# Layer 3's rank products in four partition groups side by side, with two sets of four PSUM banks

## The reference

```python
def _L3_ffn_ref(x, W, b, A, Bmat, LiMEs):     # RANK = 32, 8 experts
    scaling = ALPHA / RANK                    # 0.5
    H = jnp.einsum('btd,od->bto', x, W) + b
    z = jnp.einsum('btd,dr->btr', x, A)
    ...
    weights_full = jnp.repeat(weights, N_GRAM, axis=1)
    p_mix = jnp.einsum('bte,er->btr', weights_full, LiMEs)
    delta = jnp.einsum('btr,ro->bto', z * p_mix, Bmat) * scaling
    return H + delta
x = x + _L3_ffn_ref(_L3_cond_ref(x, itok_B_9_3973, L3_cond_conv_w), L3_ffn_W, L3_ffn_b, L3_ffn_A, L3_ffn_Bmat, L3_ffn_LiMEs)
```

## Time and profile before

| | us |
|---|---|
| median of 3 runs | 1017.63 |
| lowest and highest of them | 1017.13, 1018.17 |
| the profiled execution, device time | 1017.95 |
| its span in the trace | 1016.2 |
| TensorE busy in the span | 931.9 (92%) |
| VectorE busy | 573.8 (56%) |
| layer 3's stretch from the last rank product of the softmax on | 953.4 to 1016.2 |

### The profile page before, as it was taken

One profiled execution on the slowest core, in us unless ns is written; L12 is line 12 of the kernel. 1 busy time (PEld: TensorE's weight loads), 2 busy tenths in 40 slices (PEclk: granted clock), 3 DMA queues, 4 the chain that ended last, 5 costly groups with the idle time before them and its releaser, 6 DMA issues.

```text
span 1016.2 us, 9968 instructions
## 1 busy us (share of the span) xinstructions
PE 931.9 (92%) x3113; PEld 483.7 (48%) x3114; DVE 573.8 (56%) x883; ACT 389.2 (38%) x444; POOL 87.8 (9%) x125
## 2 busy tenths in 40 slices
PE   0499968999899999999999999999899999898998
PEld 0495428997344444444444444444244344443332
DVE  7889968887999999888840000000214224255352
ACT  2025627878777776666631010000012222241100
POOL 4100007600000000000000000022010100100000
PEclk9999998999999999999999999998899999999899
DMA  6863234560000000000010010140100000000021
GB/s 224 291 219 104 104 131 161 210 219 28 21 21 17 28 29 2 28 28 1 0 40 0 1 54 1 41 154 0 42 0 1 0 1 1 0 1 1 22 83 62
DMA packets 32591, 60.12 MB, mean 59 GB/s; under 512 B 5730, under 2 KB 7986, under 8 KB 31458
## 3 DMA queue, kind: packets, MB, share of 16 engines
q1 hardware_dynamic: 31842, 59.45, 17.3%
q0 software_dynamic: 704, 0.10, 0.1%
HBM read 51.07 MB, written 8.47 MB: 59 GB/s over the span
## 4 chain that ended last, share of the span: by engine, by line
PE 75%; DVE 17%; issue 3%; ACT 3%; ACTq 1%; DMA 1%; DVEq 1%; SPq 0%
PE ps L781 73%; DVE acc L1305 4%; DVE T L1305 3%; ACT above L632 2%; DVE W2T L1305 1%; PE ps L821 1%; ACTq L651 1%; DVE raw L1283 1%; DVE amax L1276 1%; DVE W2T L1147 1%; PE ps L1011 1%; DVE X L1372 1%; DVE W2T L1153 1%; DVE W2T L1150 0%; DVEq L1368 0%
## 5 line engine op out<-in xcount | busy, mean ns | idle before, releaser
L632 ACT ACTIVATE above<-raw,cst 128x1024 bf16<-128x1024 f32 (+2 forms) x225 | 272.4, 1232 | 143.4 <-DVE acc L1305 54.3
L781 PE MATMUL ps<-Yp,W3T 128*128 (+2 forms) x888 | 190.5, 369 | 16.8 <-DMA W3T<-in_wa 14.0
L781 PE MATMUL ps<-Up,W1T 128*128 128x512 f32 (+1 forms) x352 | 160.2, 598 | 5.5 <-DVE Yp L1406 5.0
L1305 DVE SCALAR_TENSOR_TENSOR acc<-above,acc 128x1024 f32<-128x1024 bf16 (+2 forms) x112 | 148.1, 1323 | 24.9 <-ACT above L632 15.2
L781 PEld LDWEIGHTS ps<-Yp,W3T 128*128 128x128 f32 (+1 forms) x888 | 123.8, 194 | 77.8 <-issue 75.5
L781 PE MATMUL ps<-Up,W2T 128*128 128x512 f32 (+1 forms) x352 | 158.2, 592 | 0.0
L1305 DVE SCALAR_TENSOR_TENSOR T<-above,T 128x1024 f32<-128x1024 bf16 (+1 forms) x84 | 114.2, 1359 | 13.1 <-ACT above L632 10.3
L781 PE MATMUL ps<-X,W3T 128*128 128x512 f32 (+1 forms) x256 | 116.0, 609 | 0.5 <-DVE W1T L1599 0.5
L781 PEld LDWEIGHTS ps<-Up,W1T 128*128 128x128 f32 (+1 forms) x352 | 65.7, 189 | 87.4 <-issue 86.6
L781 PEld LDWEIGHTS ps<-Up,W2T 128*128 128x128 f32 (+1 forms) x352 | 66.0, 188 | 85.1 <-issue 85.1
L781 PEld LDWEIGHTS ps<-X,W3T 128*128 128x128 f32 (+1 forms) x256 | 48.8, 194 | 66.1 <-issue 64.5
(11 more groups left out here) (289 smaller groups left out, 762.7 us busy)
## 6 DMA issues: line engine op xcount, KB each, us to landing
W3T<-in_wa SPq DMA_DIRECT2D x11, 1024.0 KB, 5.6
raw<-in_w SPq DMA_DIRECT2D x20, 256.0 KB, 3.1
W3T<-kpad SPq DMA_DIRECT2D x9, 512.0 KB, 4.4
Up<-in_xconv SPq DMA_DIRECT2D x4, 1024.0 KB, 11.3
X<-in_xT SPq DMA_DIRECT2D x1, 4096.0 KB, 22.0
xkeep<-X SPq DMA_DIRECT2D x4, 1024.0 KB, 4.5
X<-xkeep SPq DMA_DIRECT2D x4, 1024.0 KB, 9.2
W3T<-in_wa SPq DMA_DIRECT2D x5, 768.0 KB, 4.7
```

Source lines behind the costliest of these rows:

```text
L632: nc.scalar.activation(above[0:h, m % 2, 0:w], raw[0:h, u % 2, 0:w], ACT.Relu, scale=STEEP, bias=cst[0:h, C_BND + i:C_BND + i + 1]).then_i ...
L781: return nc.tensor.matmul(o, l, r, start=start, stop=stop, **kw)
L1305: V.scalar_tensor_tensor(out=ac, in0=src, scalar=float(STEPS[i]), in1=ac, op0=ALU.min, op1=ALU.add).then_inc(s["m_used"], 1)
```

## The change

- `lim2` (8 x 64, half zeros) becomes `lim4` (8 x 128): `LiMEs` four times side by side, by one copy with a broadcast. So one product of `ranks` gives the same 32 rank values in all four groups of 32 partitions. The memset of `lim2` goes.
- `bm2` becomes `bm4` (128 x 128): group oc of 32 partitions holds the columns of `Bmat` for output chunk oc, by four DMAs in place of one. The memset on GpSimd of its zero half goes.
- `zq` (128 x 2048, the first quarter of `yf`, printed as `Yp`) holds `z` four times. SyncE copies the 32 rows of `zt` into each group by four DMAs, issued once `zt` is complete and VectorE has done with the region (`a_zt`, `d_ys`).
- The four products of `ranks` run one after the other into banks 0 and 1, and VectorE makes all four blocks of `zq` in place, on 128 partitions, before it evacuates the first output. It waits for two of the products at a time.
- `lift(n)` contracts over 32 partitions, those of group oc, where it contracted over 64 before.
- Outputs use all eight banks. The order becomes lifts 0 to 3; bases 6, 7; lifts 4 to 7; bases 8 to 11; lifts 8 to 11; bases 12, 13; lifts 12, 13; base 14; lift 14; base 15; lift 15.

The diff, cut to its core:

```diff
-        BANKS3 = [4, 5, 6, 7, 2, 3]
+        BANKS3 = [4, 5, 6, 7, 2, 3, 0, 1]
...
-            sp.dma_start(bm2[RANK:, :], A["bmat"]).then_inc(s["l_bm"], 16)
+            for oc in range(DC):
+                sp.dma_start(bm4[oc * RANK:(oc + 1) * RANK, :], A["bmat"][:, oc * P:(oc + 1) * P]).then_inc(s["l_bm"], 16)
...
+            sp.wait_ge(s["a_zt"], TB)
+            sp.wait_ge(s["d_ys"], 1)
+            for oc in range(DC):
+                sp.dma_start(zq[oc * RANK:(oc + 1) * RANK, :], zt[ZA:YM, :]).then_inc(s["l_zq"], 16)
...
-            nc.gpsimd.memset(bm2[0:RANK, :], 0.0).then_inc(s["g_pad"], 1)
...
+                elif n < 8:
+                    pe.wait_ge(s["d_zp"], TB)
                 else:
-                    pe.wait_ge(s["d_o"], n - 5)
+                    pe.wait_ge(s["d_o"], n - 7)
...
-                if tb >= 2:
-                    pe.wait_ge(s["d_zp"], tb - 1)
-                mm(ps[0:YM, tb % 2, 0:256], lim2[:, :], wT[:, tb * 256:(tb + 1) * 256], True, True).then_inc(s["p_pm"], 1)
+                mm(ps[:, tb // 2, tb % 2 * 256:tb % 2 * 256 + 256], lim4[:, :], wT[:, tb * 256:(tb + 1) * 256], True, True
+                   ).then_inc(s["p_pm"], 1)
...
-                mm(ps[:, BANKS3[n % 6], :], bm2[:, oc * P:(oc + 1) * P], zp[tb % 2], False, True).then_inc(s["p_o"], 1)
+                g = slice(oc * RANK, (oc + 1) * RANK)
+                mm(ps[:, BANKS3[n % 8], :], bm4[g, :], zq[g, tok(tb)], False, True).then_inc(s["p_o"], 1)
...
+            for tb in range(TB):
+                ranks(tb)
+            pe.wait_ge(s["l_bm"], 16 * DC)
+            last_base = 5
+            for group in ([0, 1, 2, 3], [4, 5, 6, 7], [8, 9, 10, 11], [12, 13], [14], [15]):
+                while last_base < group[-1]:
+                    last_base += 1
+                    base(last_base)
+                for n in group:
+                    lift(n)
...
+            dve.wait_ge(s["l_zq"], 16 * DC)
+            for tb in range(TB):
+                dve.wait_ge(s["p_pm"], tb // 2 * 2 + 2)
+                zv = zq[:, tok(tb)].rearrange("p (a k) -> p a k", k=2)
+                V.scalar_tensor_tensor(out=zv, in0=ps[:, tb // 2, tb % 2 * 256:tb % 2 * 256 + 256].unsqueeze(2).to_broadcast(
+                    [P, 256, 2]), scalar=0.5, in1=zv, op0=ALU.mult, op1=ALU.mult).then_inc(s["d_zp"], 1)
```

More of the change, by code:

```diff
@@ L186, in build @@
         v1 = acc[0:VB, 1024:1024 + NSLOT]
-        bm2 = rawf[0:2 * RANK, 2048:2560]
+        bm4 = rawf[:, 2048:2048 + P]
         l2r = sb("l2r", [P, DC, E])
@@ L201, in build @@
         limT = sb("limT", [RANK, E])
-        lim2 = sb("lim2", [E, 2 * RANK])
+        lim4 = sb("lim4", [E, DC * RANK])
         cw = sb("cw", [P, 5])
@@ L287, in build @@
         tmp = [yf[:, 2 * TOK + i * TW:2 * TOK + (i + 1) * TW] for i in range(2)]
-        zp = [yf[0:YM, 2 * TOK + (2 + i) * TW:2 * TOK + (3 + i) * TW] for i in range(2)]
+        zq = yf[:, 0:TOK]
         results = [region[:, i * TW:(i + 1) * TW] for region, k in
@@ L299, in build @@
         s = {}
-        for n in """g_xs d_nrm m_ready m_used g_nrm d_xs p_w16 a_rk a_v2 p_rke a_kk g_pad d_wz p_va a_va p_lgt a_lgt l_l3 a_w16 d_w16 d_ak d_rmx a_fo g_x2 l_cst l_s4 l_s5 l_w0 l_u l_x l_len l_ids l_kpa l_kpb l_keep l_back l_strip0 l_strip1 l_strip2 l_strip3 l_strip4 l_raw0 l_raw1 l_wa0 l_wa1 l_wa2 l_late l_prep l_l3w
+        for n in """l_zq g_xs d_nrm m_ready m_used g_nrm d_xs p_w16 a_rk a_v2 p_rke a_kk g_pad d_wz p_va a_va p_lgt a_lgt l_l3 a_w16 d_w16 d_ak d_rmx a_fo g_x2 l_cst l_s4 l_s5 l_w0 l_u l_x l_len l_ids l_kpa l_kpb l_keep l_back l_strip0 l_strip1 l_strip2 l_strip3 l_strip4 l_raw0 l_raw1 l_wa0 l_wa1 l_wa2 l_late l_prep l_l3w
                 l_sml l_diag l_bm l_out d_sl
@@ L973, in _ @@
                     pe.wait_ge(s["d_wz"], 2)
-                    pe.wait_ge(s["g_pad"], 3)
+                    pe.wait_ge(s["g_pad"], 2)
                     for c in range(DC):
@@ L1075, in base @@
                     pe.wait_ge(s["d_yd"], n - 1)
+                elif n < 8:
+                    pe.wait_ge(s["d_zp"], TB)
                 else:
-                    pe.wait_ge(s["d_o"], n - 5)
+                    pe.wait_ge(s["d_o"], n - 7)
                 for c in range(DC):
-                    mm(ps[:, BANKS3[n % 6], :], l3w[:, c, oc * P:(oc + 1) * P], X[:, c, tok(tb)], c == 0, False)
+                    mm(ps[:, BANKS3[n % 8], :], l3w[:, c, oc * P:(oc + 1) * P], X[:, c, tok(tb)], c == 0, False)
             def spread_gate(tb):
@@ L1392, in _ @@
             link(V.reciprocal(ilen[hi64, 1:2], ilen[hi64, 0:1]))
-            link(V.memset(lim2[:, 0:RANK], 0.0))
-            link(V.tensor_copy(lim2[:, RANK:], lim[:, :]))
+            link(V.tensor_copy(lim4[:, :].rearrange("p (a r) -> p a r", a=DC), lim[:, :].unsqueeze(1).to_broadcast([E, DC, RANK])))
             def hidden(n):
@@ L1579, in _ @@
             V.tensor_tensor(tm3, tm3, ss3[:, 4, :].unsqueeze(2).to_broadcast([P, 8, E]), ALU.mult).then_inc(s["d_w3"], 1)
[L1581 to L1592, removed]
+            dve.wait_ge(s["l_zq"], 16 * DC)
[4 more added lines that the diff above has]
+                    [P, 256, 2]), scalar=0.5, in1=zv, op0=ALU.mult, op1=ALU.mult).then_inc(s["d_zp"], 1)
             for n in range(TB * DC):
                 tb, oc = n // DC, n % DC
-                if oc == 0 and tb and tb + 1 < TB:
-                    ranks(tb + 1)
                 dve.wait_ge(s["p_o"], n + 1)
-                tt(tmp[n % 2], ps[:, BANKS3[n % 6], :], G[:, tok(tb)], ALU.mult)
+                tt(tmp[n % 2], ps[:, BANKS3[n % 8], :], G[:, tok(tb)], ALU.mult)
                 V.scalar_tensor_tensor(out=results[n], in0=tmp[n % 2], scalar=b3[:, oc:oc + 1],
```

## The result

| | before | changed |
|---|---|---|
| median | 1017.38 (6 runs, 1012.48 to 1018.17) | 1005.88 (6 runs, 1003.91 to 1007.43) |
| the profiled execution, device time | 1017.95 | 1007.43 |
| its span | 1016.2 | 1005.7 |

The ratio is 0.9891, with a 95% interval of 0.9871 to 0.9912: about 11 us less. The direction was right, the size too small. The profiled execution was the slowest of the six and came out at 1007.43, where the rival "all at once" had put it at 1007.85 (10.1 off 1017.95). What the title calls rank products side by side are the lifts; the products of `ranks` still run one after the other.

What follows compares the result with a forecast made beforehand. TensorE, busy 92% of the span, was taken to bound the kernel. Cheaper lift groups, hidden rank products and a shorter slow clock end the last lift at 1004.98, not 1011.85: 1017.63 - 6.9 = 1010.7, range 1006.5 to 1014.5.

Steps and rivals of the forecast that it cites:

- all at once: Rival on the lifts: full overlap, a group or pair costs 1.05 us; 10.1 less, 1007.5; chance 0.15.
- the price of a group of lifts: Lifts in different partition groups on TensorE: partial, staggered overlap, four cost 2.64 us, a pair 1.58; chance 0.62.
- change of shape: TensorE switching between lifts and bases: each change between the two matmul shapes costs 0.19 us.
- The test on the old order: Old kernel from base 6 to the last lift, summed in the forecast's prices: 54.3 us, rows show 54.31.
- The clock: TensorE's granted clock falls to half at about 956.46 again, stretching lifts by 1.48 us and base 6 by 0.23.
- the short one: Slow-clock stretch at lifts 0 to 3 and base 6: ends within 3.4 us, by 959.9, rather than lasting 6.8.
- Up to base 6: First rank product to base 6: VectorE waits for two products, its first multiplication starts 0.4 later; base 6 starts at 959.42.
- No overlap: Rival on the lifts: groups of four cost 3.63 us, the pair 1.91; 3.6 less, 1014.0; chance 0.18 in some form.
- VectorE's evacuations: Outputs leaving the banks: 1.44 us each, 5.8 per group of four, hidden behind at least two bases, 7.3.
- the copies: Four copies of `z`, issued 917.12, wanted at 954.4: hidden; rival of late landing 1024.6, chance 0.03.
- the loads of `Bmat`: Three more loads issued at 664, about 0.6 us each, wanted at 955: cost nothing.
- the memsets: Dropped memsets of 0.51 and 0.09 us, at 722 and 252 on engines nobody waits for: save nothing.

Runs made afterwards that it cites:

- The runs with two partition groups: Changed kernel with lifts in two partition groups in place of four: neighbours in the same group 1009.07 (ratio 0.9925), alternating 1009.15 (0.9926).
- the kernel with one group: Changed kernel with all lifts contracting over partition group 0, order and banks kept: 1016.38, ratio 0.9993; run once more 1016.24, ratio 0.9990.
- the kernels with five groups: Changed kernel with lifts 12, 13, 14 as one group: 1003.15; base 6 also waiting for two multiplications: 1002.82; plus a matmul before the rank products: 1004.37.
- the last kernel: Changed kernel with lifts 12 to 14 as one group, base 6 waiting for two multiplications, and rank products on 128 partitions: 1001.26, ratio 0.9838.

## Why the prediction was wrong

**The step that failed is the price of a group of lifts.** The prediction held that a lift's second record cannot start before its first has streamed, which the rows bear out, and that the next lift's first record can at best run beside it, which is not so. It gave k + 1 steps and 0.10 for each further load, 2.64 for four and 1.58 for two; the rows show 1.07 and 1.05. The runs with two partition groups show why: a record waits only for those of its own group. The rival "all at once", to which the prediction gave a chance of 0.15, was the true case. The figure beside it from the Trainium skill, "TensorE: Matmul & The Clock Gate", section on packing small matmuls, 3.07 times for four tiles, was a little low for this kernel: 3.63 without overlap against 1.07 is 3.4 times, change of shape included.

Term by term, in the profiled execution:

| | forecast | measured |
|---|---|---|
| first rank product to base 6 | 959.42 - 953.36 = 6.06 | 957.55 - 953.77 = 3.78 |
| lifts 4 to 13, three groups | 2 x 2.64 + 1.58 = 6.86 | 1.07 + 1.07 + 1.05 = 3.19 |
| bases 6 and 7 | 3.86 + 3.63 = 7.49 | 10.11 |
| bases 8 to 13 | 6 x 3.63 = 21.78 | 13.93 + 7.07 = 21.00 |
| bases 14, 15, lifts 14, 15 | 9.43 | 9.44 |
| sum | 51.62 | 47.52 |

The first two rows come from the overlap, 5.95 too much. Of this 1.48 is slow clock that the forecast laid on lifts 0 to 3; they were over when the clock fell, and it fell on bases 6 and 7 instead. The fourth is a slip in the sum, 0.78 too much: it charged each base its change of shape, also where bases follow each other. The test on the old order could not show this, since there a lift stands between any two bases. The third row, which holds one more such 0.19, goes the other way, 2.6 too little.

**The clock was the second wrong step**, hidden in the result by the first. The forecast gave it 1.48 + 0.23 = 1.71 us; it cost 10.11 - 3.63 - 3.44 = 3.04. "The new order has no gap there, so I take the short one" failed twice: the new order did have a gap, 0.56 ahead of base 6, as the lifts were done at once and the multiplications were not (this belonged to the rival "all at once" and was in its sum); and a gap is not what decides: TensorE busy without a gap was held at 0.50 for 10.2 us in the kernel with one group, and with the gap of 0.72 and all products on 128 partitions the clock did not fall.

**Up to base 6** VectorE's first multiplication started 1.24 us after the first rank product, 0.2 later than forecast. The wait for two products was the right reading. Base 6 then waited for all four multiplications, which took 2.50 in place of 2.76.

**No overlap**, as a rival, was put at 1014.0 and came out at 1016.38 when built. With the slip taken out at its five places (0.95) and a slow stretch of 10.2 in place of 3.4 us (3.4 us of time), its 3.6 become 3.6 + 0.95 - 3.4 = 1.15, and the trace has 58.49 - 57.38 = 1.1.

**All at once** foresaw 1001.8 - 953.36 = 48.4 us for the stretch in which the trace has 47.52. The slip, which this sum has too (0.95), accounts for the difference. That the median of 1005.88 lies below the rival's 1007.5 and below the whole range is therefore in part a slip and in part the executions, since the profiled one lies inside the range.

**What held**: VectorE's evacuations, the banks, the copies (wanted 30 us after they had landed), the loads of `Bmat` and the memsets cost nothing; the price of a single lift and of a change of shape; the tail.

**What stays open.** The runs of one kernel differ by 1 to 6 us. The fourteen profiles show where part of this arises: the first rank product starts anywhere between 951.57 and 953.85, a spread of 2.3 us ahead of the change's place. What causes it is not shown; some profiles have a slow stretch more or less at 40 or 242 us, but the starts do not follow these. The slow stretch at 955 lasts equally long in both profiles of the changed kernel (6.8) and in both of the kernel with one group (10.2), and why it lasted 3.4 in the kernels with five groups is open. Why few rows go with a low clock was not tried beyond this one place. Padding with zeros changes both the rows that the array works on and the data that pass through it, and no run tells these apart. That rank products on 128 partitions suffice is shown, by the last kernel; how much the first lifts add in the changed kernel is not.

## What to carry to other kernels

Matmuls with a contraction of 32 are worth putting into four partition groups only together with an order that places them next to each other in different groups: four in a row cost what one costs, and single ones between full matmuls gain nothing. With two groups the order among four did not matter, but a pair in one group took 1.90 us, against 1.05 in two. Each lift had a PSUM bank of its own in all of these runs; anything else was not tried. Where short contractions stand together on the critical path, look at the granted clock behind them: padding the smallest ones with zeros to 128 partitions cost nothing visible here and took a slow stretch away.

## What the runs showed of the hardware

- Records of matmuls in different partition groups overtake each other: of four lifts in two groups (neighbours in the same one), four weight loads stand at the start, and four lifts take 1.93 us, so the third starts with the first, past three records that stand ahead of it. Eight weight loads of four groups take 0.31 us, where two of one group take 0.29.
- A fp32 matmul of 32 rows and 512 columns takes its two records of 0.43 us like one of 128 rows, and a change between shapes costs 0.19 us; between 128-row matmuls of different operands it costs nothing (3.44 for four lifts in place of 3.63).
- The granted clock fell to 0.50 some 3 us after the first rank product in all twelve profiles in which these products have 8 rows, for 3.4 to 10.2 us. In the two in which they have 128, with the same gap of 0.72 us ahead of them, it stayed at 1.00, once with lifts of 32 rows behind them. With products of 8 rows and lifts one after the other, it was down for 10.2 us where the lifts have 32 rows, TensorE being busy throughout, and for 3.4 where they have 128.
- Four copies from SBUF to SBUF, 256 KB each out of the same 32 partitions, landed 3.0 to 5.0 us after issue.
